# AdaLN mega-kernel: an earlier gated third in the feed-forward, and layer-norm squares on another engine

## What is computed

```python
def attn_layer(x, Wqkv, qs, ksc, Wo):          # 16 heads of 64, windows of 32 tokens
    qkv = x @ Wqkv
    q, k, v = jnp.split(qkv, 3, -1)
    q, k, v = (sh(q), sh(k), sh(v))
    q = l2norm(q) * qs
    k = l2norm(k) * ksc
    q = q * cos * scale + rotate_half(q) * sin * scale
    k = k * cos * inv + rotate_half(k) * sin * inv
    out = local_attention(q, k, v)             # softmax over this window and the one before
    return out @ Wo

def ffn_layer(x, g, bln, W1, b1, W2, b2):
    mu = x.mean(-1, keepdims=True)
    var = ((x - mu) ** 2).mean(-1, keepdims=True)
    xn = (x - mu) / jnp.sqrt(var + 1e-05) * g + bln
    hg = xn @ W1 + b1
    a, gate = jnp.split(hg, 2, -1)             # 341 inner features each
    return a * jax.nn.gelu(gate, approximate=False) @ W2 + b2

for i in range(DEPTH):
    x = attn_layer(shift_tokens(x), ...) + x
    x = ffn_layer(shift_tokens(x), ...) + x
```

## Time and profile before

| | us |
|---|---|
| median of 3 runs | 5213.91 (5198.06 to 5218.83) |
| the profiled execution | 5238.39 |
| its span, first to last instruction | 5236.6 |
| TensorE busy | 4141.3 (79%) |
| VectorE busy | 3477.7 (66%) |
| ScalarE busy | 3135.9 (60%) |
| GpSimd busy | 1083.3 (21%) |

### The profile page before, as it was taken

The page is one execution under the profiler, slowest core; times in us unless marked ns, Lnnn a source line. Parts: engine busy times, 40 slices in busy tenths (PEclk is TensorE's granted clock), DMA queues, the critical chain, the costliest instruction groups (busy, mean ns, idle before and its releaser), DMA issues. The chain is left out here.

```text
span 5236.6 us, 176300 instructions
## 1 busy us (share of the span) xinstructions
PE 4141.3 (79%) x68250; PEld 2934.0 (56%) x68250; DVE 3477.7 (66%) x6841; ACT 3135.9 (60%) x8480; POOL 1083.3 (21%) x856
## 2 busy tenths in 40 slices
PE   5665588888888888888888888888888888885368
PEld 4443466666666666665666566666666666653134
DVE  4444577767777677666777676767776777764655
ACT  2332366766666666666666676767666767662123
POOL 0000222222222222222222222222222222220012
PEclk8776799999999999999999999999999999996579
DMA  0001233333333333333333333333333333320000
GB/s 25 0 0 39 58 78 74 74 76 85 86 74 73 75 81 88 78 75 75 81 84 78 75 75 74 89 80 74 74 75 87 84 74 76 76 67 11 0 9 12
DMA packets 138442, 336.61 MB, mean 64 GB/s; under 512 B 44880, under 2 KB 46032, under 8 KB 137552
## 3 DMA queue, kind: packets, MB, share of 16 engines
q1 hardware_dynamic: 137808, 326.67, 26.5%
HBM read 22.41 MB, written 2.10 MB: 5 GB/s over the span
## 5 line engine op out<-in xcount | busy, mean ns | idle before, releaser
L990 ACT ACTIVATE loc_probs<-loc_pair,loc_ebias,loc_rnorm 128x64 f32<-128x64 f32 x3072 | 1199.5, 430 | 14.1 <-DVE loc_ebias L1150 11.7
L691 POOL TENSOR_TENSOR loc_ks<-loc_mcos,loc_swapped 128x1024 f32<-128x1024 f32 x192 | 453.3, 2361 | 1854.7 <-DVE loc_kr L1138 1363.1
L738 PE MATMUL loc_pair<-loc_hs,loc_wqk 128*128 128x256 f32 x3072 | 763.4, 392 | 40.5 <-issue 36.3
L990 ACT ACTIVATION_READ_ACCUMULATOR loc_probs<-loc_pair,loc_ebias,loc_rnorm 128x1 f32 x3072 | 710.2, 231 | 0.0
L691 POOL TENSOR_TENSOR loc_qr<-loc_mcos,loc_swapped 128x1024 f32<-128x1024 f32 x192 | 452.9, 2359 | 1210.1 <-DMA loc_swapped<-loc_msin 1210.1
L738 PEld LDWEIGHTS loc_pair<-loc_hs,loc_wqk 128*128 128x128 f32 x3072 | 572.7, 194 | 149.8 <-issue 55.0
L1090 DVE SCALAR_TENSOR_TENSOR loc_mcos<-loc_pair,loc_scal,loc_tab 128x1024 f32<-128x1024 f32 x384 | 490.9, 1278 | 197.0 <-ACT loc_sq L972 178.6
L1148 DVE TENSOR_REDUCE loc_mx<-loc_pair 128x8 f32<-128x512 f32 x384 | 264.4, 688 | 480.4 <-PE loc_pair L782 472.4
L972 ACT ACTIVATE loc_sq<-loc_pair 128x1024 f32<-128x1024 f32 x384 | 395.8, 1031 | 276.1 <-PE loc_pair L738 276.0
L1099 DVE SCALAR_TENSOR_TENSOR loc_msin<-loc_pair,loc_scal,loc_tab 128x1024 f32<-128x1024 f32 x384 | 489.9, 1276 | 33.7 <-DMA loc_swapped<-loc_msin 33.4
L782 PE MATMUL loc_pair<-loc_kr,loc_qr 64*32 64x64 f32 x24576 | 321.9, 227 | 151.8 <-issue 151.7
(11 more groups left out here) (244 smaller groups left out, 7419.5 us busy)
## 6 DMA issues: line engine op xcount, KB each, us to landing
loc_swapped<-loc_msin SPq DMA_DIRECT2D x1536, 128.0 KB, 2.3
loc_veven<-loc_vodd SPq DMA_DIRECT2D x768, 64.0 KB, 2.0
loc_veven<-loc_vodd SPq DMA_DIRECT2D x384, 128.0 KB, 2.3
loc_wqk<-wqk_dram SPq DMA_DIRECT2D x12, 512.0 KB, 3.7
loc_wv<-wv_dram SPq DMA_DIRECT2D x6, 512.0 KB, 3.3
loc_wo<-wo_dram SPq DMA_DIRECT2D x6, 512.0 KB, 4.4
x<-xT_dram SPq DMA_DIRECT2D x1, 2048.0 KB, 7.5
loc_tab<-tables_dram SPq DMA_DIRECT2D x1, 2048.0 KB, 7.7
```

What stands on the lines that cost most here:

```text
L691: nc.gpsimd.tensor_tensor(dst, mcos[i % 2][:, :], swapped[:, :], ALU.add).then_inc(rope_add, 1)
L738: ins = nc.tensor.matmul(pairs[b][:, p // 2, (p % 2) * UNIT:(p % 2 + 1) * UNIT], wqk[:, k, w:w + P], hs[u.odd][:, :], start=True, stop=True)
L990: ins = nc.scalar.activation(probs[x][:, p, hp, :], pairs[b][:, hp, p * 2 * WIN:(p + 1) * 2 * WIN], ACT.Exp, bias=ebias[x][:, k:k + 1], sc ...
```

## The change

Two edits in `local_layers`. First, the squares of the feed-forward's layer norm, until now an activation (Square) at the head of ScalarE's step, become a product `xc * xc` on VectorE, right behind `centre`, with the same two waits and the same semaphore. Second, `gated(0)` of the unit `at(5)`, until now behind `maxima(1, 0)`, `residual_ffn` and `maxima(1, 1)` on VectorE, comes directly behind `rotate_sin(2)` and ahead of all three.

```diff
             # ScalarE
-            def ln_squares(u):
-                if u is None:
-                    return
-                after(act, xc_ready, u.n)
-                after(act, var_ps, u.n - 1)
-                nc.scalar.activation(lsq[:, :], xc[:, :], ACT.Square).then_inc(lsq_ready, 1)
...
             def step(at):
-                ln_squares(at(5))
                 square(2, at(2), 2)
                 exponentials(0, 1, at(3), 1)
...
             # VectorE
+            def ln_squares(u):
+                if u is None:
+                    return
+                dve.wait_ge(xc_ready, count(u.n))
+                after(dve, var_ps, u.n - 1)
+                nc.vector.tensor_tensor(lsq[:, :], xc[:, :], xc[:, :], ALU.mult).then_inc(lsq_ready, 1)
...
             def step(at):
                 maxima(0, 1, at(3), 1)
                 centre(at(5), 4)
+                ln_squares(at(5))
                 gated(2, at(6), 3)
                 outputs(1, at(4), 0)
                 ln_rstd(at(5), 4)
                 rotate_cos(2, at(2), 2)
                 ln_normed(at(5), 4)
                 rotate_sin(2, at(2), 2)
+                gated(0, at(5), 4)
                 maxima(1, 0, at(3), 2)
                 residual_ffn(at(6), 3)
                 maxima(1, 1, at(3), 2)
-                gated(0, at(5), 4)
                 rotate_cos(3, at(2), 1)
                 rotate_sin(3, at(2), 1)
                 norms_in(at(2), 4)
```

## The result

The changed kernel takes 5234.15 us (median of 8 runs, 5222.69 to 5262.11), the one before 5213.65 beside it (8 runs, 5198.06 to 5218.83). The ratio is 1.0051, 95% interval 1.0031 to 1.0071: slower by 0.5%, where 0.9905 was forecast. The range, 5120 to 5215, does not hold it. Its profiled execution took 5262.11 us, 28 above its median, as that of the kernel before was 24.5 above: the two traces lie 23.7 us apart, the medians 20.5. A difference of 0.3 us in the mean pair of steps (some 14 us over 48 pairs) is within what executions of one kernel differ by (8 runs of the one before span 21 us).

A forecast was written before the change was run, and what follows sets the result against it. The local layers take four fifths of the span, with TensorE waiting there, largest for its own late instructions. Savings of 38 + 0 + 12 = 50 us gave 5188.4 of 5238.4 profiled (0.9905), 5164 on the median; range 5120 to 5215.

The forecast's parts named there:

- the waits: TensorE's waits in the local layers: norms for the first gated third 87.0 us, ln_var for the squares 58.7.
- the race: VectorE's last small maxima(1, 1) instruction against GpSimd's addition of rotated(2); started behind it, it takes 2.32 us, not 0.17.
- Step 1: gated(0) ahead of the second block's maxima on VectorE: norms no longer waits for it, 38 us saved, ends 0 and 69.
- The lower end, 0: Lower end of the gated(0) move's saving: the give-back at norms_across is whole.
- Step 2: Squares on VectorE: ln_var earlier, 14 us, against a later rotate_sin(2) chain, 14 us; sum 0, ends +14 and -24.
- The port: SBUF port: a VectorE instruction with two SBUF inputs, like the squares, can be held by GpSimd; priced at nothing.
- rival C: Squares on VectorE held behind GpSimd's addition once in each pair: 91 us, 5255; chance 0.03.
- The clock: After idleness at ln_var the granted clock reads 0.61 in about 15 first steps; 12 us saved, ends 0 and 25.
- A: The pair of steps gives all the gain back: 0 to 25 us saved, about 5200; chance 0.24.
- B: VectorE's addition wins the path, each step carrying 0.49 us more into rotate_sin(2): 47 us lost, 5250; chance 0.10.
- Slower: The whole kernel measurably slower than before: chance 0.13.
- inner range: The forecast time of the whole kernel, 5140 to 5190 us; chance 0.50.

The follow-up runs named there:

- e11_addition_held: The kernel before, with GpSimd's addition of rotated(2) held until the second block's maxima are through; 5195.46 us, ratio 0.9938.
- late moves: All six veven moves placed as in the kernel before, with values_out(1) waiting for all six; the kernel before takes 5213.65 us.
- early moves: Two veven moves reading the previous unit's values issued at the step's start, values_out(1) waiting for these alone; on the kernel before, ratio 0.9976.
- e7_hold_earlier: The changed kernel, with TensorE's norms held for the first of the second block's maxima, not the second; 5230.21 us, ratio 1.0046.
- e2_squares_only: The kernel before with the squares on VectorE and gated(0) at its old place; 5187.8 us, ratio 0.9946.
- e3_norms_held: The changed kernel, with TensorE's norms also waiting for the last of the second block's maxima; 5194.84 us, ratio 0.9963.
- e5_prev_after: The changed kernel with two veven moves issued at the step's start and values_out(1) waiting for these alone; 5087.56 us, ratio 0.9744.
- e10_prev_held: The changed kernel with the early moves and norms held for the second block's maxima; 5083.16 us, ratio 0.9741.

## Why the prediction was wrong

**The bound, the waits, the race: right.** `e11_addition_held` shows the race to be the cause of most of the waits of `norms` (87.0 us, 12.7 without it).

**Step 1, 38 us saved: wrong, this is the step that failed.** Measured, 32 us lost alone, 55 on top of the squares. The price of the wait was about right: taken away without moving `gated(0)` it gave 32 (`e11_addition_held`). The sentence that failed is "TensorE idles 1.16 us there instead". I read it from the 12 pairs that had no long wait, and took these for samples of what the edit would do. They are samples of a won race only: there `gated(0)` still came behind the maxima, and TensorE's stream was still let past `norms` after 13 us. The edit let it past earlier (the moved `gated(0)` ends at 10.0 us, the maxima at 13.2), which no step of the trace of before showed. The instruction packet moved from 19 or 20 us to 14, onto the SP queue's `veven` issues, and the idleness became 2.68 us (median of the first steps). So the first steps kept none of the gain (40.9 us on average against 41.0 before, where `norms` held gives 39.9). The second steps are 0.6 us longer in this trace (46.4 against 45.8), but 45.6 in that of `e7_hold_earlier`, which loses as much, so that is not shown to be part of it. I had named the queue and the chain, and counted on it only VectorE's delay, not what holds up the queue itself. The lower end, 0, rested on a whole give-back; nothing behind it excluded a loss.

**Step 2, 0: its terms read right, wrong in what it left out.** The start of the squares, 0.42 us, `ln_var` 0.92 us after the step's start, `rotate_sin(2)` at 7.47: all as said. Alone the squares gave 28 us, close to the 32 of the race by itself, so with the late moves their other terms come to little in sum; with the early moves the squares gave 92. What I wrote of the delay, that it makes "step 1's saving doubly sure, not larger", has it the wrong way round: the 0.2 us of delay won the race, and step 1 had next to nothing left to take from the wait of `norms` (29.5 us with the squares alone). Two edits that remove the same wait were to be priced as one, and then the second had mostly its risk to bring. Nor are they the same edit: the squares free VectorE of the held instruction, the moved `gated(0)` only lets TensorE pass it.

**The port.** The squares were not held (0.42), as the rows had it, and the gain of `e2_squares_only` leaves no room for rival C's 91 us. Whether they would be with a GpSimd addition beside them, no step tells: in none of the traces with the squares on VectorE does a GpSimd instruction overlap them.

**The clock, 12 us: right at `ln_var`, overlooked elsewhere.** `ln_spread` came 6.8 us after the step's start in 16 of 45 first steps before and in none now (4.7 in all 45), and the granted clock from 0 to 6 us reads 1.00 and not 0.90. (The 2.72 us of `ffn_out` was the upper end of these 16, which took 1.7 to 2.75.) The new drop stands behind the longer idleness at `norms_across` and outweighs it: 0.98 to 0.96 over the local layers. The prediction had no term for a clock that falls there.

**The rivals.** A (all given back) stopped at zero. A's signs didn't show either: first steps 40.9, not near 39.5, and second steps 46.4, not above 47. B's sign of failure, `values_out(1)` later than 17.3 us, came true (18.05 on average in first steps, 17.16 before), but not by B's mechanism: with the same VectorE order it is 17.14 once `norms` is held. Slower had 0.13, by mechanisms that were not this one. The cause that was found is none of the four rivals.

**The sum.** Kernels close to this one come nearer to the forecast of 5164: the squares alone, 5188, at the upper edge of its inner range (5140 to 5190), and the changed kernel with `norms` held, 5195, outside that and inside 5120 to 5215.

## What to carry to other kernels

Steps that happen to lack a wait are no sample of the edit that removes it: ask what else the edit sets free, above all an engine whose instructions may now run ahead of where they stood, and which transfers move with it. When two edits remove the same wait, price it once and try each alone. Where a chain through a DMA queue is the next late thing, shorten it first, by letting each consumer wait only for the moves that it needs; here that was worth more (2.6% with both edits) than both edits had promised, and it turned one of them from a loss into a gain.

## What the runs showed of the hardware

- A DMA issue on SyncE takes 0.59 us, and up to 2.4 (median 1.64 to 1.72) while a 16 KB instruction packet is under way: every one of the 344 issues above 1.2 us in the changed kernel had one, and 334 of 334 before. Not every packet does this: 261 issues with one near them weren't longer. A held 64 KB move lands 1.4 us after the end of its issue, like any other, and the one issued just before it lands after 3.2 us and not 2.0 (median of 51 in the changed kernel). The profiled time of an issue holds no data movement: the Trainium skill, "Perfetto Trace Analysis", section "DMA Instruction — HWDGE (DVE, Sync)", has it cover a wait for the descriptor generator's lock, the generation itself and the sequencer's own semaphore updates. Which of the three the packet prolongs, no row here tells.
- When such a packet comes depends on when a wait ahead in TensorE's stream is fulfilled, not only on when its products run: fulfilled at 10.0 or 11.0 us, packet at 14.2 to 14.4; at 13.2, at 19.8, with `norms` starting at 13.67 in each (`e3_norms_held`, `e7_hold_earlier`). With the early moves the two places are 13.6 and 17.8 (`e5_prev_after`, `e10_prev_held`).
- A VectorE instruction of 0.17 us, started just behind a GpSimd addition, took about 2 us in 33 of 45 first steps; holding the addition back until it is through ended that in all 45 and made the kernel 0.6% faster.
- An added wait, on something that is nearly always ready in time, made a kernel 0.9% faster.
